# A mixture-of-experts kernel: the second slot tile gathered into the experts' own buffer, and the slot table's factors in 16 bits

## What is computed

```
x = x + cross_attention_0(layernorm(x), ctx, ctx)
x = x + moe_ffn(layernorm(x))
x = x + cross_attention_1(ctx, layernorm(x))
x = x + quantized_ffn(layernorm(x))

def moe_ffn(x):                      # E = 8 experts, F = 1024, TOP_K = 2
    flat = x.reshape(-1, 256)
    logits = flat @ gate_w + gate_b
    topv, topi = lax.top_k(logits, 2)
    topw = softmax(topv)
    routing = zeros_like(logits).at[arange(T)[:, None], topi].set(topw)
    for each expert e:
        h = gelu(flat @ W1[e] + b1[e])
        final += (h @ W2[e] + b2[e]) * routing[:, e]
```

## Time and profile before

| | |
|---|---|
| median of 3 runs | 1247.54 us (1246.51 to 1251.94) |
| the profiled execution's own time | 1247.52 us |
| its span | 1245.7 us |
| PE busy | 1129.3 us, 91% of the span |
| DVE, ACT, POOL busy | 927.4, 737.3, 585.6 us |
| HBM read, written | 91.28 MB, 49.55 MB |
| routing stage | about 266.4 to 328.4 us |
| experts stage | about 328.4 to 805.0 us |

### The profile page before, as it was taken

How to read it: one execution, slowest core, us unless ns; L and a number is a source line. 1 busy time by engine, 2 the same in 40 slices (tenths; PEclk the granted TensorE clock), 3 DMA queues, 4 the chain that set the end, 5 groups by cost and what they waited for, 6 DMA issues and landing times. The chain is left out here.

```text
span 1245.7 us, 26798 instructions
## 1 busy us (share of the span) xinstructions
PE 1129.3 (91%) x9622; PEld 927.4 (74%) x9623; DVE 927.4 (74%) x1325; ACT 737.3 (59%) x976; POOL 585.6 (47%) x584
## 2 busy tenths in 40 slices
PE   3899999989699999999999999637899999999997
PEld 2566666679699999999999999525666666668886
DVE  7898999668388887888878877468888888843332
ACT  3587778855456555554655564324778777764443
POOL 1488777334488686832011000068877786201222
...
GB/s 209 173 248 223 258 226 222 129 222 299 323 138 145 157 182 215 131 139 109 42 118 42 42 51 25 58 183 198 209 211 217 197 221 179 166 37 64 73 73 36
DMA packets 120694, 192.88 MB, mean 155 GB/s; under 512 B 12128, under 2 KB 64352, under 8 KB 120480
## 3 DMA queue, kind: packets, MB, share of 16 engines
...
HBM read 91.28 MB, written 49.55 MB: 113 GB/s over the span
## 5 line engine op out<-in xcount | busy, mean ns | idle before, releaser
L2255 PE MATMUL y_ps<-e_w,hiddenT_hi 128*128 x624 | 225.2, 403 | 1.7 <-DVE slot_y L2363 1.6
L2291 ACT ACTIVATE hidden<-hidden 128x1024 f32<-128x1024 f32 x78 | 82.8, 1061 | 188.9 <-DVE hidden L2324 188.9
L2238 PE MATMUL h_ps<-kvT_hi,tile_w_hi 128*128 128x256 f32 x624 | 178.6, 286 | 4.1 <-DVE kvT_lo L2346 4.1
L2238 PE MATMUL h_ps<-kvT_lo,tile_w_hi 128*128 128x256 f32 x624 | 178.1, 285 | 0.0
L2238 PE MATMUL h_ps<-kvT_hi,tile_w_lo 128*128 128x256 f32 x624 | 178.0, 285 | 0.0
L1585 DVE TENSOR_REDUCE neg_max<-big 128x4 fp32r<-128x1024 f32 x128 | 154.6, 1222 | 30.5 <-PE big L1332 27.7
L2256 PE MATMUL y_ps<-e_w,hiddenT_lo 128*128 x624 | 175.2, 281 | 0.0
L691 DVE TENSOR_REDUCE neg_max<-big 128x4 fp32r<-128x1024 f32 x128 | 155.1, 1217 | 20.3 <-PE big L442 19.0
L601 ACT ACTIVATE probs<-big 128x1024 f32<-128x1024 f32 x128 | 130.5, 1022 | 46.3 <-PE big L453 46.1
L1492 ACT ACTIVATE probs<-big 128x1024 f32<-128x1024 f32 x128 | 130.8, 1024 | 39.8 <-PE big L1343 37.8
L2352 DVE TENSOR_TENSOR hiddenT_lo<-hidden,hiddenT_hi 128x1024 fp32r<-128x1024 f32 x78 | 100.9, 1335 | 58.2 <-ACT hiddenT_hi L2302 58.2
...
...
## 6 DMA issues: line engine op xcount, KB each, us to landing
...
e_w<-in_L_ffn_w POOLq DMA_DIRECT2D x10, 1024.0 KB, 6.7
...
vals<-in_v_wide SPq DMA_DIRECT2D x16, 512.0 KB, 4.2
vals<-v_wide SPq DMA_DIRECT2D x16, 512.0 KB, 4.6
```

Of the source, the lines that this page charges most:

```text
L2238: last = nc.tensor.matmul(h_ps[k][:, f % HF, :], w1[w][b.u][:, c, f * P:(f + 1) * P], xT[a][b.u][:, c, :], start=(n == 0), stop=(n == 3 * ...
L2255: nc.tensor.matmul(y_ps[q][:].rearrange("p s d -> p (s d)"), hT[0][o.u][:, f, rows], both, start=(f == 0), stop=False)
L2291: nc.scalar.activation(half(hidden, k), half(hidden, k), ACT.Gelu).then_inc(gelu_done, 1)
```

## The change

Tile 1 is treated like tile 0: `first_tile["x"]` and `first_tile["gathered"]` become lists of two, the two gathers write straight into the experts' buffer `slot_x1`, and neither the store to `slots_in` nor SP's load of tile 1 is left. The counts of `staged` and `x_loaded` for odd tiles go down by one. ACT, which waited for that load before it cut tile 1's weights, waits for the count of cut expert weights instead. The factors of the table are float16, in eight buffers of their own. For whole numbers up to 2048 float16 is exact, so the token numbers are shifted by -2048 in the iota, and 2048 is added when the table is converted; slots without a token now name token 2048 instead of 0. The copies of tile 0's weights no longer wait for the table and move from bodies 10 and 11 to 8 and 9.

```diff
@@ -384,8 +384,8 @@
             def make_masks():
                 nc.gpsimd.memset(const["ones"][:].bitcast(F32), 1.0).then_inc(masks_made, 1)
                 nc.gpsimd.memset(const["not_earlier"][:].bitcast(F32), -1.0).then_inc(masks_made, 1)
-                for (at, n), step, down in zip(IOTAS, (1, P, P), (0, 0, 1)):
-                    nc.gpsimd.iota(const["iotas"][:, at:at + n], pattern=[[step, n]], base=0, channel_multiplier=down,
+                for (at, n), step, down, base in zip(IOTAS, (1, P, P), (0, 0, 1), (0, 0, -(TOKENS // 2))):
+                    nc.gpsimd.iota(const["iotas"][:, at:at + n], pattern=[[step, n]], base=base, channel_multiplier=down,
                                    allow_small_or_imprecise_dtypes=True).then_inc(masks_made, 1)
                 pool.wait_ge(masks_made, 5)
                 nc.gpsimd.affine_select(out=const["not_earlier"][:], in_=const["not_earlier"][:].bitcast(F32),
@@ -1741,7 +1741,7 @@
 
 def staged_before(n):
 
-    return (n + 1) // 2 - 1
+    return n // 2 - 1
 
 
 def gather_rows(pool, const, dram, n, rows, done):
@@ -1762,7 +1762,7 @@
 
 
     for n in tiles:
-        wait(pool, staged[n % 2], (staged_before(n - STAGES) + 1) * 16 if n > STAGES else 0)
+        wait(pool, staged[n % 2], (staged_before(n - STAGES) + 1) * 16 if n >= STAGES + EARLY_TILES else 0)
         gather_rows(pool, const, dram, n, staging[n % STAGES], gathered[n % 2])
         if n > tiles[0]:
             store_rows(pool, dram, n - 1, staging, gathered, staged)
@@ -1811,10 +1811,8 @@
         v_out = [sb("v_out0", [P, QT, HEADS, VW])[:], *kv_late["v"], sb("v_out3", [P, QT, HEADS, VW])[:]]
         w2 = expert_w["w2"]
 
-        IN_W1 = 5
-        is_row, block_token = [[first_tile["w1"][s][:, k, 0:GROUP * n].rearrange("p (g n) -> p g n", n=n) for k in range(2)] +
-                               [sb(f"{name}{k}", [P, GROUP, n], F32R)[:] for k in range(2, ROWS)]
-                               for s, (name, n) in enumerate((("is_row", P), ("block_token", BLOCKS)))]
+        is_row, block_token = [[sb(f"{name}{k}", [P, GROUP, n], F16)[:] for k in range(ROWS)]
+                               for name, n in (("is_row", P), ("block_token", BLOCKS))]
         rank_ps = ctx.enter_context(nc.psum_tensor("rank_ps", [P, 512], F32))
         table_ps = ctx.enter_context(nc.psum_tensor("table_ps", [P, 512], F32))
         k_ps, v_ps = [[ctx.enter_context(nc.psum_tensor(f"{name}_ps{u}", [P, 2, SEQ], F32)) for u in range(2)] for name in ("k", "v")]
@@ -1888,9 +1886,8 @@
                 elif b == 6:
                     act.wait_ge(weights_loaded, LOADS)
                     nc.scalar.activation(w2[0][:, :, 0, :], w2[1][:, :, 0, :].bitcast(F32), ACT.Copy).then_inc(w_hi, 1)
-                elif b in (10, 11):
-                    act.wait_ge(rows_used, IN_W1 + 1)
-                    nc.scalar.activation(first_tile["w1"][0][:, b - 10, :], expert_w["w1"][:, b - 10, 0, :], ACT.Copy).then_inc(w1_hi, 1)
+                elif b in (8, 9):
+                    nc.scalar.activation(first_tile["w1"][0][:, b - 8, :], expert_w["w1"][:, b - 8, 0, :], ACT.Copy).then_inc(w1_hi, 1)
                 if b >= OUTS:
                     act.wait_ge(kv_stored[b % OUTS], (b + 1) // OUTS * 32)
                 else:
@@ -2030,14 +2027,14 @@
                 V.tensor_tensor(is_row[g % ROWS], row_iota.unsqueeze(1).to_broadcast([P, GROUP, P]),
                                 over(row_f[:, s, tiles], P), ALU.is_equal)
                 dve.wait_ge(step, n_step)
-                V.tensor_tensor(block_token[g % ROWS], block_token[g % ROWS].bitcast(F32), over(token_f[:, tiles], BLOCKS),
+                V.tensor_tensor(block_token[g % ROWS], block_token[g % ROWS], over(token_f[:, tiles], BLOCKS),
                                 ALU.mult).then_inc(rows_ready, 1)
 
             link(V.tensor_tensor(passed[:], const["slot_tile"][:].unsqueeze(2).to_broadcast([P, SLOT_TILES, EXPERTS - 1]),
                                  end[:, 0:EXPERTS - 1].unsqueeze(1).to_broadcast([P, SLOT_TILES, EXPERTS - 1]), ALU.is_ge))
             link(V.tensor_reduce(expert_f[:], passed[:], AX.X, ALU.add))
             dve.wait_ge(rows_used, GROUPS_OF_ROWS)
-            V.tensor_copy(const["token"][:], table_ps[:, 0:BLOCKS]).then_inc(token_ready, 1)
+            V.tensor_scalar(const["token"][:], table_ps[:, 0:BLOCKS], float(TOKENS // 2), None, ALU.add).then_inc(token_ready, 1)
 
             link(V.tensor_copy(const["expert"][:], expert_f[:]))
             for e in range(PLACES, EXPERTS, PLACES):
@@ -2074,11 +2071,10 @@
                 ctx_lo(n)
             pool.wait_ge(token_ready, 1)
             alone(pool)
-            gather_rows(pool, const, dram, 0, first_tile["x"], first_tile["gathered"])
-            gather_rows(pool, const, dram, 1, staging[1], gathered[1])
+            for n in range(EARLY_TILES):
+                gather_rows(pool, const, dram, n, first_tile["x"][n], first_tile["gathered"][n])
             for n in range(GATHER_AFTER + 1, TAIL_KV):
                 ctx_lo(n)
-            store_rows(pool, dram, 1, staging, gathered, staged)
 
 
 def experts(nc, const, dram, expert_w, weights_ready, early_loaded, staging, gathered, staged, first_tile, kvT, kv_late, kv_stored):
@@ -2099,7 +2095,7 @@
             return ctx.enter_context(nc.psum_tensor(name, shape, F32))
 
         HF = FC // 2
-        x = [first_tile["x"], sb("slot_x1", [P, ST, DIM])]
+        x = first_tile["x"]
 
         xT = [[w[:, u, :].rearrange("p (c n) -> p c n", c=KC) for u in range(2)] for w in kvT]
         w1 = [[first_tile["w1"][k], sb(f"tile_w1_{s}1", [P, KC, HID], F32R)] for k, s in enumerate(("hi", "lo"))]
@@ -2128,7 +2124,7 @@
 
         def loaded(n):
 
-            return n.n * 16 + 16 if n.u == 1 else n.n * 16
+            return n.n * 16
 
         class OfTiles:
 
@@ -2156,7 +2152,10 @@
         def _(sp):
             def body(b):
                 n = b.shift(1)
-                if has(n.t) and n.t0 > 0:
+                if n.t0 == 1:
+                    sp.wait_ge(early_loaded, LOADS)
+                    load_expert(sp, dram, expert_w, 2, 2, early_loaded)
+                elif has(n.t) and n.t0 > 1:
                     e = sp.value_load(const["expert"][0:1, bass.ds(n.t, 1)], min_val=0, max_val=EXPERTS - 1)
                     sp.wait_ge(weights_ready, e + 1)
                     alone(sp)
@@ -2166,9 +2165,6 @@
                     sp.wait_ge(staged[n.u], loaded(n))
                     alone(sp)
                     sp.dma_start(x[n.u][:], tiled(dram["slots_in"], n.t)).then_inc(x_loaded[n.u], 16)
-                    if n.t0 == 1:
-                        sp.wait_ge(early_loaded, LOADS)
-                        load_expert(sp, dram, expert_w, 2, 2, early_loaded)
             run_bodies(sp, body, first, loop_first, loop_end, end)
             for u in range(2):
                 sp.wait_ge(y_stored[u], (SLOT_TILES + 1 - u) // 2 * 16)
@@ -2212,8 +2208,8 @@
             places = OfTiles(pe, "place", PLACES)
 
             def turn_x(n):
-                if n.t0 == 0:
-                    pe.wait_ge(first_tile["gathered"], ST * 16)
+                if n.t0 < EARLY_TILES:
+                    pe.wait_ge(first_tile["gathered"][n.t0], ST * 16)
                 else:
                     pe.wait_ge(x_loaded[n.u], loaded(n))
 
@@ -2279,7 +2275,11 @@
                 if has(n.t) and n.t0 > 0:
                     places.read(n)
                     place = places.of(n)
-                    act.wait_ge(x_loaded[n.u], loaded(n))
+                    if n.t0 == 1:
+                        e = act.value_load(const["expert"][0:1, 1:2], min_val=0, max_val=EXPERTS - 1)
+                        act.wait_ge(weights_ready, e + 1)
+                    else:
+                        act.wait_ge(x_loaded[n.u], loaded(n))
 
                     wait(act, h_filled, (n.t - 1) * 2)
                     alone(act)
@@ -2419,8 +2419,8 @@
             gathered, staged = [[sem(f"{name}{u}") for u in range(2)] for name in ("slots_gathered", "slots_staged")]
             staging = [mb(f"staging{k}", [P, ST, DIM]) for k in range(STAGES)]
             first_tile = {
-                "x": mb("slot_x0", [P, ST, DIM]), "w1": [mb(f"tile_w1_{s}0", [P, KC, HID], F32R) for s in ("hi", "lo")],
-                "gathered": sem("first_tile_gathered"), "w1_hi": sem("tile_w1_hi"), "w1_ready": sem("tile_w1_ready"),
+                "x": [mb(f"slot_x{n}", [P, ST, DIM]) for n in range(EARLY_TILES)], "w1": [mb(f"tile_w1_{s}0", [P, KC, HID], F32R) for s in ("hi", "lo")],
+                "gathered": [sem(f"tile{n}_gathered") for n in range(EARLY_TILES)], "w1_hi": sem("tile_w1_hi"), "w1_ready": sem("tile_w1_ready"),
             }
             hidden, y = mb("hidden", [P, FC, SLOT_ROWS]), [mb(f"slot_y{u}", [P, ST, DIM]) for u in range(2)]
             kv_late = {
```

## The result

The changed kernel takes **1245.74 us** (median of 20 runs, 1237.89 to 1248.37) against 1247.79 (20 runs, 1245.83 to 1251.94) for the kernel before on the same chips: ratio 0.9976, 95% interval 0.9964 to 0.9987. That is 2.05 us gained where 7.5 were forecast, and the time lies outside the forecast range. The profiled execution took 1246.3 us, its span is 1244.4.

What follows compares the result with a forecast made beforehand. The prediction took TensorE (PE), busy 91% of the span, as the bound. Its terms, 4.4 + 3.0 + 0.3 - 0.2 = 7.5 us off 1247.52, gave 1240.0 us, range 1236.2 to 1244.8.

Steps and rivals of the forecast that it cites:

- Part 1: End of routing: without tile 1's store POOL's drain ends before SP's, so the block is released 4.4 us sooner.
- Rival 1: End of routing: POOL's drain doesn't go with the store but waits for gathers or something else; 1244.4 us, chance 0.10.
- a drain above 5 us: Sign of a wrong forecast: POOL's drain at routing's end, expected under 3 us, still taking more than 5.
- Part 2: Table matmuls in routing: 16-bit factors cut the pitch from 102 to 52 ns; 3.0 us gained, bounds 0 and 4.2.
- rival 5: Table in routing: DVE's 16-bit writes take longer and the table waits for DVE; 1258.3 us, chance 0.03.
- Part 3: First two tiles: 0.3 us off the kvT_lo wait, 0.2 lost as DVE waits 0.8 for V's store.
- Rival 3: Tile 0: K and V stores hold DVE 3 us, as gathers of tiles 2 and 3 run beside; 1242.3, chance 0.08.
- ACT's part: First two tiles: ACT cuts tile 1's weights from about release + 3 to release + 5 us, not waiting for its load.
- Costed at nothing: Effects given no time, among them expert 2's load waiting for expert 1's weights, and gathers from tile 2 shifting with the release.
- Rival 4: Expert tiles: POOL's cut of expert 1 collides with DVE elsewhere, costing 1.9 us; 1241.9 us, chance 0.07.
- Clock: Tiles 0 and 1: both slow-clock PE stretches stay; bounds 1.9 + 1.6 us better, 2.7 worse.
- PE had mostly idled: Reason given for PE's granted clock of 0.50 from 331.0 to 335.3 and 0.60 from 341.3 to 345.6.

Runs made afterwards that it cites:

- direct_only: Kernel before with tile 1 gathered directly into its own buffer, table factors left in 32 bits: 1249.16 us.
- f16_only: Kernel before with the 16-bit table factors and the two weight copies moved to bodies 8 and 9, tile 1 still staged: 1244.81 us.
- cut2_held: Changed kernel, with POOL waiting for the transposes of tile 4 before it cuts expert 2's weights: 1243.72 us.
- cuts_held: Changed kernel, with POOL waiting for tile 2's transposes before cutting expert 1's weights and tile 4's before expert 2's: 1240.76 us.
- late_expert2: Changed kernel with both POOL cuts held behind the transposes of tiles 2 and 4, expert 2's load issued behind slot tile 2's: 1241.90 us.
- store_wait_halves: Changed kernel, both POOL cuts held, DVE waiting ahead of each half of tile 0's hidden only for the store that used it: 1245.18 us.
- after: The changed kernel itself, against the kernel before: 1245.74 us.
- stores_first_late2: Changed kernel, last two K and V stores ahead of expert 1's weights, both POOL cuts held, expert 2's load behind slot tile 2's: 1238.51 us.

## Why the prediction was wrong

- **Part 1, 4.4 us**: right at the start of tile 0. direct_only starts it 4.52 us earlier. The reading of the drain was right in kind: it ends with the last bytes of the software queue. Rival 1's half of it holds too, since the drain waits for gathers (9.74 us in direct_only), but they end before SP, so it costs nothing. The prediction called a drain above 5 us a sign of being wrong; it came (8.32 us, from 306.1 on) and meant nothing, since the end counts and not the length. PE's idle time fell to 3.09 us (forecast 2.7).
- **Part 2, 3.0 us**: too small. A group of eight went from 0.82 us to 0.30 (285.04 - 284.74), 37 ns a matmul and not 52: 64 x (102 - 37) = 4.2 us, the upper bound. All of it is on the path: from the first group to the end of the last PE takes 17.1 us (284.74 to 301.80) where it took 21.4. The pitch agrees with the streaming of 78 columns (the 36 ns of the bound), and not with the weight load, which takes 98 ns as forecast but overlaps. SP's drain in f16_only, 319.7 against 323.9, says the same 4.2. DVE did not become the bound, so rival 5 is out. The Trainium skill (TensorE: Matmul & The Clock Gate, Back-to-back issue gap) gives 81 ns for 128 columns; the measured 37 for 78 decides against it here.
- **Part 3, "0.2 us lost"**: this is the step that failed. The DVE wait was sized at 0.8 us, from V landing 9.8 us after its issue with "both sides shift with part 2". The store was indeed issued 4.3 us earlier (318.28), but DVE is released by it at 330.94, 12.7 us behind the issue and only 1.5 us earlier than the 332.4 of before, while PE and DVE came 9.5 us earlier. It had not been counted that a transfer behind others in a full queue doesn't shift with its issue: the DMA share, 0.88 over the routing stretch before, is 0.98 now, and 1.06 at 321.5 to 325.2. Four other kernels with the same order ahead of the store agree (cut2_held, cuts_held, late_expert2, store_wait_halves): SP issued it between 317.4 and 320.1, and DVE was released by it between 329.8 and 331.6, in cut2_held (320.08, 330.04) no later than in late_expert2 (318.27, 330.07). The wait was 5.45 us. It costs 3.3 us before tile 1 (9.50 of lead at tile 0's matmuls, 6.16 at tile 1's). Rival 3 had the mechanism, at 3 us, and put it down to the gathers of tiles 2 and 3. Expert 1's weights ahead of the store are the larger part: without them it lands in 3.7 us. The gathers' share is not shown, since in that run the store (317.87 + 3.7) was all but done when they began at 321.08. In after the software queue moved 0.52 MB of the 4.31 MB between the store's issue and DVE's release; at that stretch's 342 GB/s this is 1.5 us, an estimate. The forecast of ACT's part was right: it cuts tile 1's weights at 323.06 to 325.06, and nothing there waits for a load.
- **Costed at nothing, "the gathers ... start with the release as before, and shift with it"**: they do, and POOL's cuts with them (first cut 9.6 us earlier; the second 10.7, as it began at 374.30 before). But after V's wait DVE and PE are only 5.4 us ahead, so the cuts land elsewhere in DVE's round. Rival 4 had this for expert 1's cut (1.9 us; it cost 1.0) and did not look at expert 2's, which cost 4.0: 2.3 us of PE's wait at 376.41, and then a stretch at half the clock (0.51 from 377.9 on), so that tile 4's up matmuls take 7.34 us (376.41 to 383.75) where tile 3's took 5.76 (362.10 to 367.86). The rivals were priced one at a time; they come together, since one sets the phase for the other.
- **Clock**: "leave both stretches in" was nearly right for the first, but the longer wait before tile 1 made the second worse: 25 matmuls in 5.30 us at 0.50, where before it was 23 in 4.30 at 0.60. From their first to the next turn, the up matmuls of tile 0 take 8.13 us against 7.73 before, those of tile 1 8.16 against 7.36. The prediction's reading that PE had mostly idled ahead of the second stretch was wrong: from 335.3 to 341.3 PE was busy for 4.08 us, and idle for the last 1.92.

By rows: +9.1 at tile 1, -3.7, -1.0, -4.0, and +1.2 later leaves 1.5 us, with 2.05 in the medians. With the order of SP's transfers and the place of the cuts put right (stores_first_late2) the same two parts give 8.9.
